# The second cross-attention of a fused two-layer network: four edits in its head loop and its last head

## The reference, cut to what matters

```python
q = _fq_sym(q, axis=-1)
k = _fq_sym(k, axis=-1)
v = _fq_sym(v, axis=2)                     # scale per channel, over all keys
attn = jnp.einsum('bhqd,bhkd->bhqk', q, k)
attn = jax.nn.softmax(attn.astype(jnp.float32), axis=-1)
attn = _fq_unsigned(attn, axis=-1)         # round to 0..255 by the row maximum
out = jnp.einsum('bhqk,bhkd->bhqd', attn, v)
out = jnp.transpose(out, (0, 2, 1, 3)).reshape(B, N, C)
return out @ Wp + bp                       # then added to x
```

## Time and profile before

| | us |
|---|---|
| median of 3 runs | 758.09 (756.24 to 768.75) |
| the profiled execution, its own time | 761.38 |
| its span | 759.7 |
| DVE busy over the span | 514.6 |
| ACT busy | 379.0 |
| POOL busy | 331.7 |
| PE busy | 642.3 |

### The profile page before, as it was taken

The page is one execution under the profiler, slowest core; times in us unless marked ns, Lnnn a source line. Parts: engine busy times, 40 slices in busy tenths (PEclk is TensorE's granted clock), DMA queues, the critical chain, the costliest instruction groups (busy, mean ns, idle before and its releaser), DMA issues. The chain is left out here.

```text
span 759.7 us, 13009 instructions
## 1 busy us (share of the span) xinstructions
PE 642.3 (85%) x4732; PEld 415.9 (55%) x4732; DVE 514.6 (68%) x781; ACT 379.0 (50%) x736; POOL 331.7 (44%) x263
## 2 busy tenths in 40 slices
PE   3867999975999997799965889878787869889997
PEld 1333444544777775577742455545454545567775
DVE  3368999965433324999986899999999944523222
ACT  2157855513211113255645889898888942212221
POOL 1049999952111101244432878887687750000000
PEclk9989999996999998899995577687768868999999
DMA  8837100013355522144435676668675825900000
GB/s 352 297 115 290 57 0 1 0 37 94 126 187 188 187 63 91 49 132 124 117 97 166 126 166 140 155 114 179 105 167 120 154 57 224 423 22 1 0 0 14
DMA packets 96518, 93.79 MB, mean 123 GB/s; under 512 B 69776, under 2 KB 87376, under 8 KB 92112
## 3 DMA queue, kind: packets, MB, share of 16 engines
q1 hardware_dynamic: 83920, 86.78, 40.2%
q10 hardware_dynamic: 12544, 6.29, 2.9%
HBM read 69.66 MB, written 6.62 MB: 100 GB/s over the span
## 5 line engine op out<-in xcount | busy, mean ns | idle before, releaser
L1789 DVE TENSOR_REDUCE d_nmax<-d_psum 128x1 f32<-128x1024 f32 x128 | 153.2, 1212 | 15.0 <-PE d_psum L1911 14.7
L1911 PE MATMUL d_psum<-d_kst,d_qT 96*128 96x512 bf16 x256 | 105.4, 518 | 34.5 <-DMA d_kst<-kT_scratch 16.4
L425 POOL TENSOR_TENSOR b_h<-b_h,b_cb 128x1024 f32<-128x1024 f32 x32 | 87.6, 2739 | 6.8 <-DVE b_h L475 6.3
L1765 POOL TENSOR_SCALAR d_rounded<-w_early,d_lift 128x1024 f16<-128x1024 f32 x64 | 71.6, 1118 | 29.8 <-ACT d_lift L1866 25.1
L1862 ACT ACTIVATE d_e<-d_psum,d_nmax 128x1024 f32<-128x1024 f32 x64 | 71.1, 1116 | 18.9 <-DVE d_nmax L1789 18.2
L1862 ACT ACTIVATE w_early<-d_psum,d_nmax 128x1024 f32<-128x1024 f32 x64 | 71.3, 1114 | 12.8 <-DVE d_nmax L1789 12.8
L1765 POOL TENSOR_SCALAR d_rounded<-d_e,d_lift 128x1024 f16<-128x1024 f32 x64 | 72.9, 1139 | 11.0 <-ACT d_lift L1866 3.0
L475 DVE TENSOR_TENSOR_SCAN b_h<-b_dA,b_psum 128x1024 f32<-128x1024 f32 x32 | 73.1, 2285 | 2.5 <-ACT b_dA L530 2.0
L1575 PE MATMUL k_psum<-k_wkv,k_ctxT 128*128 128x256 f32 x256 | 67.6, 397 | 5.2 <-issue 5.2
L530 ACT ACTIVATE b_dA<-b_dtT,b_A 128x248 f32<-128x248 f32 x128 | 53.7, 490 | 33.1 <-DVE b_h L475 28.1
L1933 PEld LDWEIGHTS d_psum<-d_ident_f,d_rounded 128*128 128x128 f16 x512 | 45.7, 124 | 36.9 <-issue 24.5
(11 more groups left out here) (397 smaller groups left out, 1206.7 us busy)
## 6 DMA issues: line engine op xcount, KB each, us to landing
d_kst<-kT_scratch SPq DMA_DIRECT2D x96, 128.0 KB, 2.7
w<-in_w SPq DMA_DIRECT2D x8, 1088.0 KB, 20.3
b_cb<-c_scratch SPq DMA_DIRECT2D x4, 2048.0 KB, 7.1
w_early<-in_w0gu SPq DMA_DIRECT2D x8, 768.0 KB, 4.7
w_late<-in_w0gu SPq DMA_DIRECT2D x8, 768.0 KB, 4.6
kT_scratch<-k_kT ACTq DMA_DIRECT2D x16, 384.0 KB, 2.8
a_ctxT<-in_ctxT SPq DMA_DIRECT2D x2, 2048.0 KB, 12.0
a_ctx<-in_ctx SPq DMA_DIRECT2D x2, 2048.0 KB, 20.5
```

What stands on the lines that cost most here:

```text
L425: nc.gpsimd.tensor_tensor(hv, hv, cv, ALU.mult).then_inc(hc_ready, 1)
L1765: nc.gpsimd.tensor_scalar(tile_of(r, j), e[j], lift[t][:, f:f + 1], HALF_ULP_ONE, ALU.mult, ALU.add).then_inc(r_ready, 1)
L1789: nc.vector.tensor_reduce(nm[:, t, m:m + 1, f:f + 1], quarter(m, j).unsqueeze(1), AX.X, ALU.max, negate=True).then_inc(nm_ready, 1)
L1911: last = nc.tensor.matmul(quarter(m, j)[:, b * 512:(b + 1) * 512], qT[0:QROWS, m:m + 1, t * P:(t + 1) * P], kst[m % 2][0:QROWS, at:at + 51 ...
```

## The change

It has four parts, all in `xattn1_stage`.

1. `round_values` moves from behind the sixth search to behind the eighth and its row minimum.
2. The row minimum is no longer a scan of two SBUF tiles but a `tensor_scalar` of one (plus log 255, minimum with 1e30) whose accumulated output is the minimum. `log255` and its two memsets go.
3. The DMA transpose of tile t = 0 becomes four, each issued as soon as POOL has rounded its quarter, each with a semaphore of its own, for which POOL waits before it overwrites that quarter in the next head.
4. The last head is shared out. POOL rounds only its first six pieces; DVE rounds the seventh, ACT the eighth. The scales of all heads are worked out, and 15 of the 16 heads scaled, before the last head's product is copied; only 16 columns per tile are left to scale behind it. The transposes, copies and projections of `o` go by halves of 128 channels. The keep-warm matmuls go.

```diff
@@ SP @@
                 def turn_unit(m, t):
-                    sp.wait_ge(r_ready, m * APH + (t + 1) * QT)
                     if m >= 2:
                         sp.wait_ge(av_done, m + 1)
-                    sp.dma_start_transpose(pT[m % 2][:, t, :, :], r[t][:, :]).then_inc(turned_in[t], 16)
+                    for f in range(QT):
+                        sp.wait_ge(r_ready, m * APH + t * QT + f + 1)
+                        sp.dma_start_transpose(pT[m % 2][:, t, f * CPQ:(f + 1) * CPQ, :],
+                                               r[t][:, f * QUARTER:(f + 1) * QUARTER]).then_inc(turned_in[f], 16)
@@ POOL @@
+                        if m == H - 1 and j in (APH - 2, APH - 1):
+                            continue
...
-                        elif m >= 1 and f == 0:
-                            pool.wait_ge(turned_in[t], m * 16)
+                        elif m >= 1:
+                            pool.wait_ge(turned_in[f], m * 16)
@@ DVE @@
-                        nc.vector.tensor_tensor_scan(mb[:, t, m, :], nm[:, t, m, :], log255[:, :], NEG, ALU.min,
-                                                     ALU.add).then_inc(mb_ready, 1)
+                        nc.vector.tensor_scalar(raised[:, :], nm[:, t, m, :], LOG255, NEG, ALU.add, ALU.min,
+                                                accum_out=mb[:, t, m, QT - 1:QT]).then_inc(mb_ready, 1)
...
+                def scale_back(half):
+                    rows = slice(0, (H - 1) * HD) if half == 0 else head_cols(H - 1)
+                    return nc.vector.tensor_tensor(o[:, :, rows], o[:, :, rows], back[:, :, rows], ALU.mult)
+
+                def round_last():
+                    dve.wait_ge(mb_ready, H * TC)
+                    nc.vector.tensor_tensor(dm[:, :, :, :], mb[:, :, :, QT - 1:QT].to_broadcast([P, TC, H, QT]), nm[:, :, :, :],
+                                            ALU.subtract).then_inc(dm_ready, 1)
+                    j = APH - 2
+                    dve.wait_ge(lift_ready, H * TC)
+                    dve.wait_ge(e_ready, H * APH)
+                    dve.wait_ge(turn_psum, (H - 1) * len(BY_PE))
+                    nc.vector.tensor_scalar(tile_of(r, j), e[j], lift[1][:, QT - 2:QT - 1], HALF_ULP_ONE, ALU.mult,
+                                            ALU.add).then_inc(r_vector, 1)
+
+                def sum_up():
+                    dve.wait_ge(de_ready, 1)
+                    step(nc.vector.tensor_tensor(zp[:, :, :, :], zp[:, :, :, :], dm[:, :, :, :], ALU.mult))
+                    step(nc.vector.tensor_reduce(rz[:, :, :], zp[:, :, :, :], AX.X, ALU.add))
+                    step(nc.vector.reciprocal(rz[:, :, :], rz[:, :, :]))
+                    step(nc.vector.tensor_tensor(back[:, :, :].rearrange("p t (h e) -> p t h e", e=HD),
+                                                 sv[:, :].rearrange("p (h e) -> p h e", e=HD).unsqueeze(1).to_broadcast([P, TC, H, HD]),
+                                                 rz[:, :, :].unsqueeze(3).to_broadcast([P, TC, H, HD]), ALU.mult))
+
                 def vector_head(m):
+                    if m == H:
+                        round_last()
+                    if m == H + 1:
+                        sum_up()
+                        dve.wait_ge(o_ready, H - 1)
+                        scale_back(0).then_inc(o_scaled, 1)
...
-                        if j == 5 and m < H:
+                        if j == APH - 1 and m < H:
                             round_values(m)
@@ ACT @@
+                def round_last():
+                    j = APH - 1
...
+                    nc.scalar.activation(tile_of(r, j).unsqueeze(1), e[j].unsqueeze(1), ACT.Copy, bias=HALF_ULP_ONE,
+                                         scale=lift[1][:, QT - 1:QT]).then_inc(r_scalar, 1)
+                    act.wait_ge(dm_ready, 1)
+                    nc.scalar.activation(dm[:, :, :, :], dm[:, :, :, :], ACT.Exp).then_inc(de_ready, 1)
@@ PE @@
                 rounds(tensor_head)
-                keep_warm(nc, g, ps[:, 2, :], 3)
-                pe.wait_ge(o_scaled, 1)
-                transpose_tokens(nc, ps[:, 0, :], o, ident).then_inc(oT_psum, 1)
-                keep_warm(nc, g, ps[:, 2, :], 2)
...
+                pe.wait_ge(w_in, 32)
+                turn_out(0)
+                turn_out(1)
+                project(0)
+                project(1).then_inc(out_psum, 1)
```

More of the change, by code:

```diff
@@ L1631, in xattn1_stage @@
         mb = sb("d_mm_log255", [P, TC, H, QT])
-        log255 = sb("d_log255", [P, QT])
+        raised = sb("d_nmax_raised", [P, QT])
         rz = sb("d_rz", [P, TC, H])
@@ L1646, in xattn1_stage @@
         o = sb("d_o", [P, TC, D])
+        back = sb("d_back_scale", [P, TC, D])
         oT = sb("d_oT", [P, KC, T])
@@ L1664, in xattn1_stage @@
         turn_psum = sem("d_turn_psum")
-        turned_in = [sem(f"d_turned_in{t}") for t in range(TC)]
+        turned_in = [sem(f"d_turned_in{f}") for f in range(QT)]
         even_copied = sem("d_even_copied")
@@ L1845, in _ @@
                 dve.wait_ge(out_psum, 1)
-                step(nc.vector.tensor_tensor(x[:, :, :], x[:, :, :], ps[:, 1, :].rearrange("p (t c) -> p t c", t=TC), ALU.add))
+                step(nc.vector.tensor_tensor(x[:, :, :], x[:, :, :], ps[:, 1:1 + TC, 0:D], ALU.add))
             @block.scalar
@@ L1883, in _ @@
                 rounds(scalar_head)
-                act.wait_ge(dm_ready, 1)
-                nc.scalar.activation(dm[:, :, :, :], dm[:, :, :, :], ACT.Exp).then_inc(de_ready, 1)
-                act.wait_ge(oT_psum, 1)
-                nc.scalar.activation(oT[:, :, :], ps[:, 0, :].rearrange("p (k t) -> p k t", k=KC),
-                                     ACT.Copy).then_inc(oT_ready, 1)
+                for k in range(KC):
+                    keep_oT(k)
             @block.tensor
@@ L1929, in turn @@
                 def turn(m, j):
-                    pe.wait_ge(r_ready, m * APH + (j + 1 - APH))
+                    if m == H and j == APH - 2:
+                        pe.wait_ge(r_vector, 1)
+                    elif m == H and j == APH - 1:
+                        pe.wait_ge(r_scalar, 1)
+                    else:
+                        pe.wait_ge(r_ready, m * APH + (j + 1 - APH))
                     bank_free(m, j)
@@ L1942, in values @@
                     if t in BY_DMA:
-                        pe.wait_ge(turned_in[t], m * 16 - 16)
+                        for f in range(QT):
+                            pe.wait_ge(turned_in[f], m * 16 - 16)
                     else:
@@ L1964, in tensor_head, with turn_out, project @@
                             values(m, 0)
-                rounds(tensor_head)
-                keep_warm(nc, g, ps[:, 2, :], 3)
-                pe.wait_ge(o_scaled, 1)
-                transpose_tokens(nc, ps[:, 0, :], o, ident).then_inc(oT_psum, 1)
-                keep_warm(nc, g, ps[:, 2, :], 2)
-                pe.wait_ge(oT_ready, 1)
-                for t in range(TC):
-                    for k in range(KC):
-                        last = nc.tensor.matmul(ps[:, 1, t * D:(t + 1) * D], oT[:, k, t * P:(t + 1) * P], wp[:, k, :],
-                                                start=(k == 0), stop=(k == KC - 1))
-                last.then_inc(out_psum, 1)
+                def turn_out(k):
+                    pe.wait_ge(o_scaled, k + 1)
+                    for t in range(TC):
+                        last = nc.tensor.transpose(ps[:, 3 * k, t * P:(t + 1) * P], o[:, t, k * P:(k + 1) * P], ident[:, :])
+                    last.then_inc(oT_psum, 1)
+                def project(k):
+                    pe.wait_ge(oT_ready, k + 1)
+                    for t in range(TC):
+                        last = nc.tensor.matmul(ps[:, 1 + t, 0:D], oT[:, k, t * P:(t + 1) * P], wp[:, k, :],
+                                                start=(k == 0), stop=(k == KC - 1))
+                    return last
+                rounds(tensor_head)
+                pe.wait_ge(w_in, 32)
[3 more added lines that the diff above has]
+                project(1).then_inc(out_psum, 1)
 def rms_norm(nc, dve, step, out, in_, ss, root_ready, count, done):
```

25 lines of the change are left out of this document (12 added, 13 removed).

## The result

| | before | changed |
|---|---|---|
| median (us) | 758.79 (756.24 to 768.75, 4 runs) | 738.13 (730.86 to 742.89, 4 runs) |
| ratio, 95% interval | | 0.9721 (0.9656 to 0.9786) |
| the profiled execution, span | 761.38, 759.7 | 730.86, 729.2 |

What follows compares the result with a forecast made beforehand. DVE bounds the loop, with waits for POOL. Heads falling from 13.04 to 12.2 us save 11.8 over 14, the stage's end 4.7: together 16.5 us, from 758.09 to 741.6 us, range 731 to 755.

Steps and rivals of the forecast that it cites:

- the rivals: Four other outcomes: PE or ACT takes over 0.28, accumulated form still waits 0.08, SP bounds 0.06, everything fits 0.08.
- fixed cost of about 2 us per DMA: If it stood in SP's queue, a transpose quarter would take 2.9 us there; the prediction's trace reading put it outside.
- The read of the accumulator: Second step of the new row minimum on DVE: 0 to 0.19 us each, taken as 0.07, twice a head.
- The rounding's wait b: Values' rounding on DVE waits for POOL: b = 12.65 - P for head length P, giving 0.62 us.
- DVE's floor and idle: DVE's head without waits, 11.27 us, plus 0.17 for remaining idle for PE and later second factors.
- five signs of being right: Ranges named beforehand for row minimum, values' roundings, head length, SP's quarters and the stage's last matmul.
- this lead: With four transposes, keys come 1.7 us sooner in each head; costed at nothing in the steady heads.
- The four quarters: Four transposes on SP's queue: 1.82 us each, 7.3 us a head, against 5.40 for the whole transpose.
- The rival in which SP bounds: Quarters over 2.1 us let SP's queue set the head; at 3 us each, 793 us in total; chance 0.06.
- Part 4, 4.7 forecast: End of the stage after the last search: +15.4 against +19.8 us, 4.4 saved, taken as 4.7, between 3.2 and 6.5.
- Nothing gained by sharing: Last head's rounding shared by DVE, ACT and POOL: last copy still ends near +9.1 us after the last search.
- the 6.5 us of the bound: Upper bound of the gain at the stage's end, if the projection all runs at the high clock.

Runs made afterwards that it cites:

- e11: Changed kernel with the values rounded behind the sixth search again and the row minimum as a scan again; median 754.99 us, ratio 0.9887.
- e5: Changed kernel with the values rounded behind the sixth search again; median 731.79 us, ratio 0.9608.
- e3: Kernel before with only the DMA transpose split into four quarters; median 760.15 us, ratio 1.0058.
- e7: Changed kernel with one whole transpose behind all four quarters again; median 742.56 us, ratio 0.9748.
- e12: Changed kernel with the old end of the stage back, the other three parts kept; median 743.14 us, ratio 0.9773.
- e4: Kernel before with only the new end of the stage (part 4); median 757.64 us, ratio 0.9996.
- e8: Changed kernel with POOL rounding all eight pieces of the last head, rest of part 4 kept; median 737.25 us, ratio 0.9680.
- e6: Changed kernel with the row minimum as a scan of two SBUF tiles again; median 739.33 us, ratio 0.9725.
- e10: Changed kernel with keep-warm matmuls back, three ahead of the output transposes and two behind them; median 736.03 us, ratio 0.9737.

## Why the prediction was right, and where its terms were off

**The mechanism held.** DVE bounds the loop, its waits are for POOL's instruction under way, and the accumulated row minimum takes no part in them. None of the rivals was needed: it didn't wait (0.158 us at most in 32), SP was held 9.7 us a head (5.98 + 3.75), DVE's idle time for PE fell to 0.23 us a head, and ACT's head of 11.4 still fits into 11.80. The fixed cost of about 2 us per DMA that the prediction weighed there from the Trainium skill ("DMA: Bandwidth & Descriptors", "Anatomy of one DMA") was fitted on DMAs issued by GpSimd, which these are not, and it doesn't stand in SP's queue: most quarters held it 1.33 us in all. By the Trainium skill ("SBUF — State Buffer", "Who interferes with whom") that row minimum was free of the exclusion; the rows agree for all 32.

**The sum of the loop, 14 x 1.24 = 17.3 us against 11.8.** The head was forecast at 12.2 and took 11.80. Term by term:

- *The read of the accumulator*, 0.07 twice, is nothing. What stands behind it starts 1.33 us after the search ahead (502.20 to 503.53), and behind a fast scan 1.32 (e11, 533.21 to 534.53). The new form costs what the fast scan did.
- *The rounding's wait b*, 0.62 forecast, 0.38 measured (5.3/14). For equal heads of 11.80 the formula gives 12.65 - 11.80 = 0.85, and the rows show 0.86 (1.28 - 0.42) at 503.53. What the formula left out is that the wait ends with POOL's piece, not with its run of four. When the heads get shorter, the border between third and fourth piece comes to stand there, and the wait falls to 0.01 at 491.69. So b rises and falls like a saw with the length of a head, and its mean is under half of 0.85. The heads, 11.1 to 12.7 us long, follow it in the main: the six with a wait under 0.2 us took 11.55 on the mean, the other eight 11.99.
- *DVE's floor and idle*: 11.80 - 0.38 - 0.23 (3.2/14) = 11.19, against 11.27; idle 0.23 against 0.17.

11.19 + 0.38 + 0.23 = 11.80, and 0.14 + 0.24 + 0.08 - 0.06 = 0.40 is the miss. Of the prediction's five signs of being right, one held as stated (no row minimum over 0.3 us) and four fell outside: heads of 11.80 (12.0 to 12.4 named), quarters of 1.33 at the median (1.4 to 2.0), the last matmul at +14.8 (15 to 16), and roundings that took 0.42 to 1.28 us (0.4 to 1.1).

**Part 1 as a step of its own failed.** The prediction gave it no separate price and never asked what the rounding would cost in its old place. e5 shows that with part 2 in, it would have waited as long there (5.1 us in sum). The two places meet the same POOL, and a shorter head moves POOL's runs in either.

**Part 3, "I cost it at nothing in the steady heads", "this lead is what keeps them in time at 12.2".** Both halves are right as sentences. Alone it gave nothing (e3), and without it the head stops at 12.50 (e7). But a reader of the sum would have thought it worth nothing, and it carries 9.8 us of the profiled loop (2.0 to 5.2 of the whole time, intervals overlapping). The four quarters were taken as 7.3 us, 1.82 each with 0.63 of it fixed; they took 5.98 a head, 1.50 each on the mean, against 5.19 for the whole. So what cutting adds is 0.8 us a head, not 1.9 (7.3 - 5.40). The rival in which SP bounds was thus far off.

**Part 4, 4.7 forecast, 4.95 in the profile, 3.8 by e12's profile.** The whole time confirms neither: 3.9 by the ratios of e12, with intervals that overlap, and at most 2.9 by e4. Nothing gained by sharing: right (e8). Last copy +9.1: right to a tenth. Product's copy +10.9: it came at +10.4. Projection at the low clock, added at +14.9 against +15.4: right in this execution, though e6 and e10 found the high clock, which the 6.5 us of the bound had provided for. Keep-warm matmuls at nothing: not contradicted, and not shown.

**What was luck.** The range of 731 to 755 held, but the median of 738.13 lay 3.5 us under the forecast, and nearly all errors of the loop went one way: the read, the saw and the floor. Two profiled executions differ by 8 us and more ahead of the stage, so one whole time can't confirm a term of 2 us. The heads, counted apart, do so to about 2 us (the same loop gave 11.66 to 11.80, times 14), and the waits and steps inside them more closely.

## What to carry to other kernels

Before pricing an edit, list the bounds that stand close together: an edit that takes only one of them away shows nothing by itself (part 3), and two that break the same rhythm don't add (parts 1 and 2). Price a set of edits as a set, and take each back singly from the full version, since only that shows what is needed. A wait between two engines for a shared resource ends with the instruction under way on the other, so its size depends on where that instruction's border falls, and changes as the loop gets shorter.
